# Cross-attention block: scores with keys on partitions, and the maximum subtracted by VectorE and GpSimd in halves

## The chip, the cores and the metric

The kernel runs on one core of a Trainium2 chip. The metric is device time in microseconds (us) from the first to the last instruction of one execution; the median of several runs is compared.

## What is computed

A gated cross-attention block followed by a small mixture of low-rank experts, all in fp32. Eight batches of 56 query tokens attend to 1500 context tokens each; 32 query heads of 128 share 8 key/value heads, four to one.

```python
q = layernorm(x) @ wq                    # (8, 56, 32 x 128), rotary
k = ctx @ wk;  v = ctx @ wv              # (8, 1500, 8 x 128), k rotary; each used by 4 query heads
raw = einsum('bhqd,bhkd->bhqk', q, k) / sqrt(128)
attn = softmax(raw + mask)               # mask (8, 56, 1500)
x = x + tanh(g_xattn) * (attn @ v) @ wo
x = x + tanh(g_ffn) * experts(layernorm(x))
```

## The kernel before

Every fp32 product is made of rounded operands: an operand is split into a high half (ScalarE's copy to fp32r) and a low half (VectorE or GpSimd: the value minus the high half), and three matmul passes, `PASSES`, sum high x high, low x high and high x low. So a matrix that TensorE made and TensorE will read costs one copy on ScalarE and one subtraction on VectorE.

The program has three parts: the queries of all heads (kept in DRAM), the attention, the output and the experts. The attention is 64 steps: batches b of 0 to 7, and in each the key/value heads g of 0 to 7. A step does the softmax and the weighing of its own head, and makes the keys of the next head and values for a pair of heads. The order of the tasks within a step is written out by hand for each engine, in `PE_STEP`, `ACT_STEP` and `DVE_STEP` (lines 66 to 99), for steps of the kinds even, odd, turn (the last head of a batch, which also turns the context of the next batch) and last. The tasks:

- K: keys of the next head, three chunks of 500, on TensorE (L805, 12 matmuls of 500 columns a chunk); ScalarE swaps the halves (swap, L715), VectorE does the rotary cosine, sine and add (cos L938, sin L942, rot L948), ScalarE the high half (L720), GpSimd the low half (`k_low`, L673).
- V: values of two heads, in items of two tiles of 125 keys (L821, 24 matmuls of 256 columns an item), high half on ScalarE (L734), low half on VectorE (L962). An even step does two items, an odd one and the turn four.
- S: scores, the queries as the stationary operand, so that 112 query rows (two heads) lie on partitions and 500 keys on columns: six items of three matmuls (L845). VectorE adds the mask and takes the maximum in one instruction (mask, L1002), reduces the three maxima of a half (max, L1007); ScalarE subtracts the maximum, exponentiates and sums in one instruction over 1500 keys (exp, L760), two a step.
- T: the probabilities have queries on partitions, but weighing needs keys there, so TensorE turns them, six items of four transposes (L857); ScalarE takes the high half (L785) and VectorE the low half (L1027), both from the PSUM bank `t_banks`, a ring of two.
- PV: six items of four matmuls (L874), high values times both halves of the probabilities (448 columns) and low values times the high half (224); ScalarE and VectorE add the two parts (out, L770 and L1033).
- norm: VectorE multiplies by the inverse of the sums (L987), which SyncE has stored to DRAM and loaded back over all partitions; the result goes to `attn`, of two slots, and SyncE stores it.
- C: in the turn, twelve items of four transposes of the next batch's context (L832), high half on ScalarE (L724), low half on VectorE (L953).

Each engine runs its list in order; waits are on semaphores (`t_ready`, `t_free`, `sv_free`, `k_lo` and others). TensorE waits for `k_lo` ahead of scores, `t_free` ahead of turns and of weighing.

## Time and profile before

| | |
|---|---|
| median of 3 runs | 2007.14 us (2006.73 to 2007.7) |
| span of the profiled execution | 2005.4 us |
| TensorE busy | 1976.7 us (99%) |
| VectorE busy | 1235.0 us (62%) |
| ScalarE busy | 1034.3 us (52%) |
| GpSimd busy | 311.6 us (16%) |
| the 64 steps | from 124.0 us to about 1905 us of the span |

In the profile's rows PE is TensorE's matmuls, PEld its weight loads, DVE VectorE, ACT ScalarE, POOL GpSimd and SP SyncE. Matmuls are pipelined, so their busy times overlap, and the distance between two starts is what one costs. The same holds in small for VectorE: the next instruction starts a little before the last one's end. What lies between the span and the profiled execution's full time is not shown; the span is 1.7 us below the median.

### The profile page before, as it was taken

What the parts mean: (1) busy time and instruction counts of PE and PEld (TensorE: products, weight loads), DVE (VectorE), ACT (ScalarE), POOL (GpSimd) and SP (SyncE); (2) the same over time, 40 slices, a digit from 0 to 9 for tenths busy, and PEclk for the clock granted to TensorE, in tenths of its full rate; (3) what the DMA queues carried; (4) which work ended last, traced back from release to release, by engine and by line L of the source; (5) the groups of instructions that cost most, each with busy time, mean ns of one, the idle gap of its engine ahead of it and who ended that gap; (6) DMA issues with size and microseconds to landing.
All of it is one profiled execution on the core that took longest, in us unless ns stands there. A gap on an engine that the chain in (4) does not pass through costs nothing. (4 is left out here: it accounts for less than half of the span.)

```text
span 2005.4 us, 32965 instructions
## 1 busy us (share of the span) xinstructions
PE 1976.7 (99%) x12404; PEld 1775.9 (89%) x12404; DVE 1235.0 (62%) x2639; ACT 1034.3 (52%) x1754; POOL 311.6 (16%) x227
## 2 busy tenths in 40 slices
PE   7999999999999999999999999999999999999998
PEld 7989889988899988998899988998899998999786
DVE  6766556666666666666666666666665666566544
ACT  6655555554545555555644555455554555455532
POOL 5511111111111111111111111111111111111200
PEclk9999999999999999999999999999999999999998
DMA  7611212111211212221111112221111112121270
GB/s 227 248 56 35 35 18 44 35 31 20 43 10 33 36 17 44 35 35 20 39 19 25 35 20 41 36 35 20 39 25 26 28 20 41 36 33 15 48 263 19
DMA packets 74904, 94.41 MB, mean 47 GB/s; under 512 B 22692, under 2 KB 49444, under 8 KB 74760
## 3 DMA queue, kind: packets, MB, share of 16 engines
q1 hardware_dynamic: 73752, 86.01, 20.4%
q10 hardware_dynamic: 1008, 6.42, 0.8%
q8 instruction: 97, 1.59, 0.4%
q14 instruction: 47, 0.39, 0.1%
HBM read 76.64 MB, written 15.77 MB: 46 GB/s over the span
## 5 line engine op out<-in xcount | busy, mean ns | idle before, releaser
L673 POOL TENSOR_TENSOR k_lo<-k_work,k_hi 128x500 fp32r<-128x500 f32 x192 | 244.1, 1285 | 1541.0 <-ACT k_hi L720 1513.3
L821 PE MATMUL low_banks<-wv_hi,cT_hi 128*125 128x256 f32 x1536 | 443.1, 288 | 0.0
L821 PE MATMUL low_banks<-wv_hi,cT_lo 128*125 128x256 f32 x1536 | 431.0, 281 | 0.0
L821 PE MATMUL low_banks<-wv_lo,cT_hi 128*125 128x256 f32 x1536 | 430.9, 281 | 0.0
L1027 DVE TENSOR_TENSOR pT<-t_banks,pT 125x448 fp32r<-125x448 f32 x384 | 236.0, 622 | 242.8 <-ACT pT L785 242.8
L1002 DVE CUSTOM_DVE_ANT_0 prob<-low_banks,mask_t 112x500 f32<-112x500 f32 x384 | 259.1, 678 | 178.2 <-PE low_banks L845 176.9
L785 ACT ACTIVATE pT<-t_banks 125x448 fp32r<-125x448 f32 x384 | 205.1, 543 | 309.2 <-PE t_banks L857 308.2
L760 ACT ACTIVATE prob<-prob,neg_max 112x1500 f32<-112x1500 f32 x128 | 198.6, 1552 | 289.7 <-DVE neg_max L1007 288.9
L805 PE MATMUL low_banks<-cT_hi,wk_hi 128*128 128x500 f32 x768 | 312.0, 406 | 0.0
L805 PE MATMUL low_banks<-cT_hi,wk_lo 128*128 128x500 f32 x768 | 298.6, 389 | 0.0
L805 PE MATMUL low_banks<-cT_lo,wk_hi 128*128 128x500 f32 x768 | 298.3, 388 | 0.0
L821 PEld LDWEIGHTS low_banks<-wv_hi,cT_hi 128*125 128x125 f32 x1536 | 285.1, 186 | 4.3
L821 PEld LDWEIGHTS low_banks<-wv_hi,cT_lo 128*125 128x125 f32 x1536 | 285.8, 186 | 2.7
L821 PEld LDWEIGHTS low_banks<-wv_lo,cT_hi 128*125 128x125 f32 x1536 | 285.2, 186 | 0.0
L874 PE MATMUL o_banks<-pT,v_hi 125*128 125x448 f32 x768 | 272.4, 387 | 1.8 <-DVE pT L1027 0.7
L715 ACT ACTIVATE k_work<-low_banks 64x500 f32<-64x500 f32 x384 | 223.6, 582 | 14.4 <-PE low_banks L805 5.8
L857 PE MATMUL t_banks<-ident,prob 112*125 112x112 f32 x1536 | 220.6, 270 | 0.9 <-DVE pT L1027 0.9
L857 PEld LDWEIGHTS t_banks<-ident,prob 112*125 112x125 f32 x1536 | 207.0, 188 | 14.3 <-DVE pT L1027 1.0
L962 DVE TENSOR_TENSOR v_lo<-low_banks,v_hi 125x512 fp32r<-125x512 f32 x192 | 132.2, 689 | 137.0 <-ACT v_hi L734 137.0
L734 ACT ACTIVATE v_hi<-low_banks 125x512 fp32r<-125x512 f32 x192 | 114.3, 595 | 192.5 <-PE low_banks L821 192.3
L874 PE MATMUL o_banks<-pT,v_lo 125*128 125x224 f32 x768 | 193.5, 265 | 0.0
L805 PEld LDWEIGHTS low_banks<-cT_lo,wk_hi 128*128 128x128 f32 x768 | 144.5, 188 | 29.9
(136 smaller groups left out, 2910.2 us busy)
## 6 DMA issues: line engine op xcount, KB each, us to landing
stage<-in_ctx_dram SPq DMA_DIRECT2D x72, 250.0 KB
attn_by_head<-attn SPq DMA_DIRECT2D x65, 112.0 KB, 1.7
wq_raw<-in_L_xattn_wq_dram SPq DMA_DIRECT2D x7, 1024.0 KB, 7.2
q_raw<-q_by_head SPq DMA_DIRECT2D x64, 112.0 KB, 4.9
inv_b<-inv_by_head SPq DMA_DIRECT2D x64, 112.0 KB, 5.1
head_rows<-in_ctx_dram SPq DMA_DIRECT2D x24, 250.0 KB
mask_t<-in_mask_BxSxS_ff_dram SPq DMA_DIRECT2D x16, 328.1 KB
stage<-in_L_xattn_wo_dram SPq DMA_DIRECT2D x4, 1024.0 KB, 7.3
```

What stands on the lines that cost most here:

```text
L673: nc.gpsimd.tensor_tensor(k[1][:, c * SC:(c + 1) * SC], k_rot[:, s], f32(k[0][:, c * SC:(c + 1) * SC]), ALU.subtract).then_inc(k_lo, 1)
L715: nc.scalar.activation(k_swap[lo * HALF:(lo + 1) * HALF, s], k_banks[(1 - lo) * HALF:(2 - lo) * HALF, s, 0:SC], ACT.Copy).then_inc(k_swapp ...
L734: nc.scalar.activation(v[0][:, 2 * m:2 * m + 2, :], sv_banks[0:ST, m % 2, :].rearrange("p (t n) -> p t n", t=2), ACT.Copy).then_inc(v_hi, 1)
L760: nc.scalar.activation(prob[n][:, :], prob[n][:, :], ACT.Exp, bias=neg_max[:, n:n + 1], accum_out=row_sum[:, n:n + 1]).then_inc(p_ready, 1)
L785: nc.scalar.activation(pT[:, n % PT_SLOTS, :, 0, :], t_banks[0:ST, t_bank, 0:2 * GQ].rearrange("p (t n) -> p t n", t=2), ACT.Copy).then_in ...
L805: mm = nc.tensor.matmul(k_banks[:, s, 0:SC], w[0][a][:, d, g * DH:(g + 1) * DH], cT[m][:, d, c * SC:(c + 1) * SC], start=(d == 0 and n == ...
L821: mm = nc.tensor.matmul(sv_banks[0:ST, m % 2, t * PAIR:(t + 1) * PAIR], cT[a][:, d, tile * ST:(tile + 1) * ST], w[1][mv][:, d, g * DH:g * ...
L857: mm = nc.tensor.transpose(t_banks[0:ST, s, col:col + ROWS], prob[h][:, (2 * j + t) * ST:(2 * j + t + 1) * ST], ident[0:ROWS, 0:ROWS])
L874: mm = nc.tensor.matmul(o_banks[:, g % 2, 0:(2 - a) * GQ], v[a][:, 2 * j + t, (g % 2) * DH:(g % 2 + 1) * DH], probs, start=(first and a == ...
L962: nc.vector.tensor_tensor(v[1][:, 2 * m:2 * m + 2, :], sv_banks[0:ST, m % 2, :].rearrange("p (t n) -> p t n", t=2), f32(v[0][:, 2 * m:2 * ...
L1002: nc.vector.tensor_tensor_reduce(prob[h][:, c * SC:(c + 1) * SC], sv_banks[0:ROWS, n % 2, 0:SC], mask_t[:, c * SC:(c + 1) * SC], 1.0, LOWE ...
L1027: nc.vector.tensor_tensor(pT[:, n % PT_SLOTS, :, 1, :], t_banks[0:ST, t_bank, 0:2 * GQ].rearrange("p (t n) -> p t n", t=2), f32(pT[:, n % ...
```

## The change

Scores are computed with the keys as the stationary operand, so that 125 keys lie on partitions and the 4 x 56 queries on columns. The probabilities come out as weighing needs them, and the turns T are gone. In exchange the maximum and the sum run across partitions.

- Scores: twelve key tiles of three matmuls of 224 columns, two tiles an item, in `t_banks`. VectorE adds the mask out of PSUM into the new SBUF tile `weights`. The mask is turned too (two items B a batch, three transposes each, and a copy by VectorE into `mask_keys`).
- Maximum: VectorE takes it tile by tile (max1 to max5, 448 columns each, both operands in SBUF), then of the two halves (half, 224). TensorE turns the result (MT), VectorE reduces it (rows), TensorE turns it back spread over the partitions (MB), ScalarE copies it to SBUF (maxb).
- Subtraction: six pieces of 448 columns; VectorE does 0 to 2, GpSimd 3 to 5 (`V_SUBS = 3`).
- Exponential on ScalarE, six pieces of 448, without sum. GpSimd adds the pieces up (add1 to add5, total); TensorE turns the sums in the next step (SUM) and VectorE reduces and inverts them (inv).
- High and low halves of the probabilities (T in ScalarE's and VectorE's lists) now read `weights` in SBUF.
- `o_banks` goes from two banks to one, `attn` is gone: `o_sum` is normalised in place and stored, and ScalarE's "out" waits for that store. The values have their own ring (`v_banks`), and weighing counts its pieces in `p_weighed`.
- GpSimd has a list of its own, `POOL_STEP`. The last step's output projection is cut into heads.

The core of the diff:

```diff
 PE_STEP = {
-    "even": ("K00 S0 S1 K01 K02 S2 S3 K03 K10 S4 S5 K11 K12 K13 V40 K20 T0 T1 K21 V41 K22 T2 K23 PV0 V50 T3 PV1 T4 "
-             "V51 PV2 T5 PV3 PV4 PV5"),
+    "even": ("S0 S1 K00 S2 S3 SUM S4 S5 K01 K02 K03 K10 K11 K12 MT K13 MB V40 V41 V50 V51 PV0 K20 K21 K22 PV1 PV2 "
+             "K23 PV3 PV4 PV5"),
...
 ACT_STEP = {
-    "even": "exp0 swap0 exp1 swap1 Q K0 T0 T1 V4 T2 swap2 T3 T4 V5 T5 K1 K2 out",
+    "even": "swap0 Q swap1 maxb exp0 T0 exp1 exp2 T1 V4 T2 V5 exp3 exp4 T3 K0 T4 exp5 T5 swap2 K1 out K2",
...
 DVE_STEP = {
-    "even": ("mask0 mask1 mask2 mask3 max0 mask4 mask5 max1 cos0 sin0 rot0 cos1 T0 T1 sin1 rot1 norm T2 Q V4 inv cos2 T3 "
-             "sin2 T4 rot2 V5 T5 out"),
+    "even": ("mask0 mask1 max1 mask2 mask3 max2 mask4 mask5 max3 max4 max5 half inv rows cos0 Q cos1 sub0 sub1 "
+             "sub2 T0 sin0 sin1 T1 rot0 V4 V5 T2 rot1 T3 T4 T5 norm cos2 sin2 out rot2"),
...
+POOL_STEP = {
+    "odd": "sub3 sub4 sub5 add1 klo0 add2 add3 klo1 add4 add5 total klo2",
+    "even": "sub3 sub4 sub5 add1 add2 add3 add4 klo0 klo1 add5 total klo2",
...
+                if what == "sub":
+                    if j == V_SUBS:
+                        pool.wait_ge(max_copied, n + 1)
+                    nc.gpsimd.tensor_tensor(bank_weights(j), bank_weights(j), max_b[:, None, :].broadcast_to([ST, 2, GQ]),
+                                            ALU.subtract).then_inc(p_shifted, 1)
+                if what == "add":
+                    pool.wait_ge(p_exp, n * PT + (j + 1))
...
+                    nc.gpsimd.tensor_tensor(key_sum[:, :, :], so_far, bank_weights(j), ALU.add).then_inc(p_added, 1)
...
+                if what == "exp":
...
+                    nc.scalar.activation(bank_weights(j), bank_weights(j), ACT.Exp).then_inc(p_exp, 1)
+                if what == "T":
+                    act.wait_ge(p_exp, n * PT + (j + 1))
+                    if n * PT + j >= PT_SLOTS:
+                        act.wait_ge(p_weighed, n * PT + (j + 1 - PT_SLOTS))
+                    nc.scalar.activation(pT[:, j % PT_SLOTS, :, 0, :], bank_weights(j), ACT.Copy).then_inc(p_hi, 1)
...
                 if what == "out":
-                    act.wait_ge(o_ready, b * HKV + (g + 1))
-                    nc.scalar.activation(o_lo[:, :], o_banks[:, g % 2, GQ:2 * GQ], ACT.Copy).then_inc(o_lo_copied, 1)
+                    act.wait_ge(p_weighed, (n + 1) * PT)
+                    act.wait_ge(attn_stored[(n + 1) % 2], 16 * (n // 2 + 2))
+                    nc.scalar.activation(o_sum[:, :], o_bank[:, GQ:2 * GQ], ACT.Copy).then_inc(o_copied, 1)
...
+            for t in range(2):
+                tile = slice((2 * j + t) * ST, (2 * j + t + 1) * ST)
+                for n, (a, m) in enumerate(PASSES):
+                    mm = nc.tensor.matmul(t_banks[0:ST, item % 2, t * GQ:(t + 1) * GQ], k[a][:, tile], q[m][:, :],
+                                          start=(n == 0), stop=(n == len(PASSES) - 1))
...
+            nc.vector.tensor_tensor(bank_weights(j).rearrange(four, h=REP),
+                                    t_banks[0:ST, item % 2, 0:2 * GQ].rearrange("p (t h s) -> p t h s", t=2, h=REP),
+                                    mask_keys[:, j, :, None, :].broadcast_to([ST, 2, REP, SQ]), ALU.add).then_inc(t_free, 1)
...
+            so_far = bank_weights(0) if j == 1 else key_max[:, :, :]
+            nc.vector.tensor_tensor(key_max[:, :, :], so_far, bank_weights(j), ALU.max).then_inc(max_steps, 1)
...
+        def shift(n, j):
+            if j == 0:
+                dve.wait_ge(max_copied, n + 1)
+            nc.vector.tensor_tensor(bank_weights(j), bank_weights(j), max_b[:, None, :].broadcast_to([ST, 2, GQ]),
+                                    ALU.subtract).then_inc(p_shifted_first, 1)
...
                 if what == "T":
-                    dve.wait_ge(t_hi, t_item(b, g, n, last) + 1)
-                    nc.vector.tensor_tensor(pT[:, n % PT_SLOTS, :, 1, :],
-                                            t_banks[0:ST, t_bank, 0:2 * GQ].rearrange("p (t n) -> p t n", t=2),
-                                            f32(pT[:, n % PT_SLOTS, :, 0, :]), ALU.subtract).then_inc(t_free, 1)
+                    dve.wait_ge(p_hi, n * PT + (j + 1))
+                    nc.vector.tensor_tensor(pT[:, j % PT_SLOTS, :, 1, :], bank_weights(j), f32(pT[:, j % PT_SLOTS, :, 0, :]),
+                                            ALU.subtract).then_inc(p_lo, 1)
```

## Rows read from the trace of the kernel before

**Rows 1.** The page, busy time of each engine and its share.
```profile
PE 1976.7 (99%) x12404; PEld 1775.9 (89%) x12404; DVE 1235.0 (62%) x2639; ACT 1034.3 (52%) x1754; POOL 311.6 (16%) x227
```

**Rows 2.** Windows: stretch, us, busy us of PE, PEld, DVE, ACT, POOL, PEclk, DMA share, GB/s.
```profile
682.00:705.90 23.90, 23.86 (x148) 21.23 (x147) 15.85 (x36) 12.94 (x22) 2.80 (x3) 1.00 0.02 6
705.90:736.60 30.70, 30.70 (x202) 28.08 (x202) 17.46 (x39) 14.85 (x26) 4.68 (x5) 1.00 0.22 28
761.30:796.90 35.60, 35.60 (x244) 32.20 (x243) 23.92 (x51) 20.46 (x37) 4.45 (x4) 1.00 0.29 58
572.70:796.90 224.20, 224.06 (x1441) 202.10 (x1440) 139.96 (x309) 117.22 (x204) 30.59 (x25) 1.00 0.17 30
```

**Rows 3.** Timeline of TensorE: start, duration, line, shapes.
```profile
715.02 0.39 PE L805 MATMUL low_banks<-cT_hi,wk_lo 128*128 128x500 f32 x1
715.25 0.39 PE L805 MATMUL low_banks<-cT_lo,wk_hi 128*128 128x500 f32 x1
...
721.53 0.59 PE L857 MATMUL t_banks<-ident,prob 112*125 112x112 f32 x4
721.89 0.36 PE L821 MATMUL low_banks<-wv_hi,cT_hi 128*125 128x256 f32 x1
722.09 0.28 PE L821 MATMUL low_banks<-wv_hi,cT_lo 128*125 128x256 f32 x1
722.21 0.28 PE L821 MATMUL low_banks<-wv_lo,cT_hi 128*125 128x256 f32 x1
...
724.34 0.38 PE L874 MATMUL o_banks<-pT,v_hi 125*128 125x448 f32 x1
724.55 0.27 PE L874 MATMUL o_banks<-pT,v_lo 125*128 125x224 f32 x1
724.65 0.29 PE L821 MATMUL low_banks<-wv_hi,cT_hi 128*125 128x256 f32 x1
```

**Rows 4.** Groups by line and shape: count, busy us, mean ns, idle before; VectorE, ScalarE.
```profile
L1027 DVE TENSOR_TENSOR pT<-t_banks,pT 125x448 fp32r<-125x448 f32 x384 | 236.0, 622 | 242.8 <-ACT pT L785 242.8
L785 ACT ACTIVATE pT<-t_banks 125x448 fp32r<-125x448 f32 x384 | 205.1, 543 | 309.2 <-PE t_banks L857 308.2
L962 DVE TENSOR_TENSOR v_lo<-low_banks,v_hi 125x512 fp32r<-125x512 f32 x192 | 132.2, 689 | 137.0 <-ACT v_hi L734 137.0
L948 DVE TENSOR_TENSOR k_work<-k_work 128x500 f32<-128x500 f32 x192 | 129.6, 675 | 11.6 <-DVE k_work L942 1.9
L1033 DVE TENSOR_TENSOR o_sum<-o_banks,o_lo 128x224 f32<-128x224 f32 x64 | 25.1, 392 | 56.1 <-ACT o_lo L770 56.1
```

**Rows 5.** The same view, GpSimd's instructions of 448 columns.
```profile
L685 POOL TENSOR_TENSOR cT_lo<-head_rows,cT_hi 128x448 fp32r<-128x448 f32 x4 | 4.5, 1151 | 0.0
```

**Rows 6.** Timeline of VectorE and GpSimd around 569 us, and a k_lo that met nothing.
```profile
569.22 0.62 DVE L1027 TENSOR_TENSOR pT<-t_banks,pT 125x448 fp32r<-125x448 f32 x1 [1.85 <-ACT pT L785]
569.76 0.67 DVE L948 TENSOR_TENSOR k_work<-k_work 128x500 f32<-128x500 f32 x1
570.35 0.68 DVE L962 TENSOR_TENSOR v_lo<-low_banks,v_hi 125x512 fp32r<-125x512 f32 x1
...
569.77 1.78 POOL L673 TENSOR_TENSOR k_lo<-k_work,k_hi 128x500 fp32r<-128x500 f32 x1 [10.95 <-ACT k_hi L720]
...
626.81 1.27 POOL L673 TENSOR_TENSOR k_lo<-k_work,k_hi 128x500 fp32r<-128x500 f32 x1 [4.39 <-ACT k_hi L720]
```

**Rows 7.** Timeline of VectorE and GpSimd around 1879 us.
```profile
1879.42 0.90 DVE L948 TENSOR_TENSOR k_work<-k_work 128x500 f32<-128x500 f32 x1
...
1878.49 1.29 POOL L681 TENSOR_TENSOR wk_lo<-stage,wk_hi 128x512 fp32r<-128x512 f32 x1 [7.62 <-ACT wk_hi L1059]
...
1879.73 2.98 POOL L681 TENSOR_TENSOR wk_lo<-stage,wk_hi 128x512 fp32r<-128x512 f32 x2
```

**Rows 8.** DMA issues of the page (KB each, us to landing), and the last step's window.
```profile
attn_by_head<-attn SPq DMA_DIRECT2D x65, 112.0 KB, 1.7
...
1882.20:1905.00 22.80, 18.47 (x84) 14.72 (x84) 10.70 (x22) 8.97 (x11) 8.59 (x8) 0.93 0.44 100
```

More of the change, by code:

```diff
@@ L90 @@
 DVE_STEP = {
[8 rows of a table removed]
[16 rows of a table added]
+}
+POOL_STEP = {
[7 rows of a table added]
 }
 def step_kind(g, last):
-    return ("last" if last else "turn") if g == HKV - 1 else ("odd" if g % 2 else "even")
-def act_kind(g, last):
-    return "pre" if last and g == HKV - 2 else step_kind(g, last)
+    if last and g >= HKV - 2:
+        return "last" if g == HKV - 1 else "pre_last"
+    return ("zero", "odd", "even", "odd", "even", "odd", "pre", "turn")[g]
 def tasks(order):
@@ L706, in _ @@
+        with pool.Fori(0, B - 1) as b:
+            for g in range(HKV):
+                step(b, g, False)
+        for g in range(HKV):
+            step(B - 1, g, True)
     @block.scalar
@@ L869, in weigh @@
+        def weigh(n, j):
+            if j == 0 and n:
+                pe.wait_ge(o_free, n)
+            pe.wait_ge(p_lo, n * PT + (j + 1))
+            if n % 2 == 0:
+                pe.wait_ge(v_free, v_item(n // 2, j) + (RING + 1))
             for t in range(2):
@@ L1178, in _ @@
         with sp.Fori(1, pairs - 1) as i:
-            output_loads(sp, shared, wo, attn_dram, i, sp_passed)
+            for u in range(2):
+                output_load(sp, shared, wo, attn_dram, i, u, sp_passed)
         for t in range(NTT):
```

478 lines of the change are left out of this document (274 added, 204 removed), and 58 rows, old and new, of tables (ACT_STEP, DVE_STEP, PE_STEP, POOL_STEP).

## The prediction

> **What bounds the kernel now.** I read the page's totals first. TensorE is busy 99% of the span, VectorE 62%, ScalarE 52%, GpSimd 16% [rows 1]. Then I cut one batch into its steps [rows 2]: an even step takes 23.9 us, an odd one 30.7 us (it has four projections of V, the even one two), the turn 35.6 us, and a batch 224.2 us, which is 28.0 us a step. In each window TensorE is busy from end to end and VectorE for 16 to 24 us. So TensorE's queue is the bound, and what it saves is worth its full size until another engine takes over. The reader is to ask two things: how much leaves TensorE, and whether VectorE and GpSimd, which receive it, still fit into a step.
>
> **TensorE.** The busy times of the page overlap, so I price matmuls by the distance of their starts [rows 3]. 500 moving columns cost 0.23 us, 448 cost 0.21, 256 cost 0.12 and 224 cost 0.10 to 0.105. Four turns of probabilities take 0.36 us, and the matmul behind them starts 0.08 late (0.20 to the next one instead of 0.12).
> - Removed: six groups of four turns, 6 x 0.44 = 2.64 us a step.
> - Scores: 18 matmuls of 500 columns (4.09 us) become 36 of 224. Two of 224 in a row do not occur before; the bounds are 0.105 (the 224 row) and 0.118 (the 256 row, which loads 125 weight columns too). I take 0.105: 3.78 us, a gain of 0.31; at 0.118 it is a loss of 0.16.
> - Added: three pairs of turns (maximum out, maximum back, sums), each 0.18 + 0.08 = 0.26, together 0.78 us; two pieces of mask a batch, some 0.7 us, 5.6 us in all.
> - Sum: 2.64 + 0.31 - 0.78 = 2.17 us a step. Over 64 steps that is 139 us, less 5.6 = 133. If TensorE stayed the bound, the span of 2005.4 us would become 1872.
>
> TensorE's need is then 21.8 us for an even step, 28.5 for an odd one and 33.5 for the turn.
>
> **ScalarE.** Two exponentials of 1500 columns become six of 448, and six high halves now read SBUF. The row for 448 columns is 543 ns [rows 4]; bounded by that and by VectorE's 622 for the same size, 12 such cost 6.5 to 7.5 us, and with swaps, K, V and the rest ScalarE needs 13 to 15 us. It has room. Its new waits matter more: "out" now waits until the previous attention tile has been stored, because o_sum serves both; K2 is queued behind it, and so is VectorE's "out", with the next step's masks behind that. The store takes 1.7 us from issue to landing [rows 8].
>
> **VectorE, alone.** Its instructions start 0.54 us apart where one lasts 0.62, and 0.59 where one lasts 0.67 [rows 6], so an instruction's price is its mean [rows 4] less 0.08. An even step then has 20 instructions of 448 columns (6 masks, 5 maxima, 3 subtractions, 6 low halves) = 10.8 us; nine of 500 (cosine, sine, add) = 5.3; two of V = 1.2; four of 224 = 1.2; the two reductions of 250 columns lie between the rows for 224 and 448, with the reciprocal 0.8. Together 19.3 us. An odd step has two more of V, 20.5; the turn has twelve context halves (7.1) and two mask copies (0.9) more, 28.5. Taken alone it fits under TensorE.
>
> **GpSimd, alone.** A 448-column instruction takes 1.15 us [rows 5], a k_lo 1.27 [rows 6]. A step now has three subtractions, five adds, one total (half the columns, an estimate of 0.6) and three k_lo: 9.2 + 0.6 + 3.8 = 13.6 us, where before it was 3.8. Alone it fits too.
>
> **VectorE and GpSimd together.** This is the step that decides. In [rows 6] VectorE starts the rotary add (both inputs in SBUF) at 569.76 and GpSimd starts a k_lo at 569.77: that k_lo takes 1.78 us instead of 1.27, so it stood still for 0.51 us, nearly all of VectorE's 0.67. VectorE's next instruction, V's low half with one input in PSUM, runs beside GpSimd at its usual 0.68. In [rows 7] it is the other way round: GpSimd started at 1878.49 and ends at 1879.78, VectorE's add is issued at 1879.42 and takes 0.90 instead of 0.67, then GpSimd's next one, issued at 1879.73, stands until that add is through. So when both read two operands from SBUF one waits for the other, and where both are waiting they alternate. Before, only the rotary sine and add, q_lo and the normalisation could meet a k_lo, and they rarely do: the add's mean is 675 ns, and one pattern a batch shows the 1.78.
>
> The Trainium skill, "SBUF — State Buffer", section "Who interferes with whom", says the same in general: a VectorE instruction with two SBUF inputs contends with a GpSimd instruction that reads SBUF, and whichever starts first keeps the shared port for its whole length. By that rule all the instructions counted next are hit; the two rows of this trace agree.
>
> After the change the instructions of VectorE with two SBUF inputs are 5 maxima, the halving, 3 subtractions, 6 low halves (they read PSUM before), 3 sines, 3 adds, q_lo and the normalisation: 23 a step. By the 0.51 for 500 columns they hold GpSimd off for 14 x 0.46 + 6 x 0.51 + 3 x 0.23 = 10.2 us. GpSimd lets go some 0.14 us ahead of its end (1879.78 less 1879.65, at which the held add must have begun), so its twelve hold VectorE off for 13.6 - 1.7 = 11.9 us. The two sum to 22.1 us, already as long as TensorE's even step, at no idle and no hand-over.
>
> How much falls on VectorE's time depends on what else it does meanwhile. Its work with a PSUM input is 7.3 us, but masks, which are most of it, come before the maximum is known, when GpSimd has nearly nothing ready. From the first subtraction to the end of an even step stand only one cosine, two of V and "out", and with one operation left over into the masks' stretch I let 2.7 us of GpSimd run beside them. The other 9.2 us delay VectorE: 19.3 + 9.2 = 28.5, and 1.0 for waits on ScalarE (out behind the store, the late swap): 29.5 us. Walking the order gives the same: with the maximum spread 10.5 us into the step, eight VectorE instructions alternate with eight of GpSimd at 1.5 us a pair, reach 22.3, and the remaining ten of VectorE with four of GpSimd end near 30. An odd step has 1.2 us more of V as cover, so 20.5 + 8.0 + 1.0 = 29.5, near enough to TensorE's 28.5 that I take 30.3. The turn: 28.5 + 6.0 + 1.5 = 36.0. A batch is 4 x 29.5 + 3 x 30.3 + 36.0 = 245, or 30.6 us a step against 28.0. 64 x 2.6 = 166 us more: 2005.4 + 166 = 2171. The median of the runs shown, 2007.1, lies 1.7 above the span, so 2173.
>
> **DMAs and SyncE.** The order of SyncE's queue changes (the inverse of the sums one step later, the store last, masks in pieces of 500 bytes). VectorE inverts within the first third of a step and normalises in the last, so I cost this at nothing; its cover is that distance. Only the last step normalises ahead of its subtractions; a stall of a few us there, once, lies inside the rounding.
>
> **The rivals.** All are conditions on the same meeting of two engines.
> - Alternating as above, 2173 (2080 to 2290): chance 0.60. For it: both orders of meeting in rows, and 23 + 12 instructions a step that meet.
> - Partly covered: only half of the 9.2 falls on VectorE, since GpSimd idles for exponentials and catches up under V and masks. Even 26, odd 29.2, turn 35: 28.3 a step, 2025. Chance 0.13.
> - Not slower: VectorE's queue is never given up between two of its own, and GpSimd runs only in VectorE's gaps. Then the held time is packed. Place: the stretch behind the spread maximum; price: 22.1 us plus some 2.5 of hand-over and idle, 24.7 for an even step, TensorE's 28.8 and 34 for the others, 27.4 a step, 64 x 0.6 = 40 us less: 1967. It decides from the point where VectorE's delay in an even step falls below 23.9 - 19.3 = 4.6 us, half of what I put. Against it: [rows 7], where GpSimd gets the turn right after VectorE. Chance 0.14.
> - The meeting costs nearly nothing and TensorE stays the bound: 1874. Against it stand the same rows. Chance 0.06.
> - Worse than 2290: waits on the store and on k_lo chain from step to step, and TensorE, waiting a quarter of the time, is granted less clock, as in the stretch that is 81% busy and shows 0.93 [rows 8]. Even 33, odd 33.5, turn 39: 33.9 a step, 2385. Chance 0.07.
> - That the change does not do what it says (no gain on TensorE at all, 0.118 for scores): 0.5 us a step on TensorE, hidden in the forecast since TensorE is not the bound there.
>
> **How the numbers follow.** The likeliest case gives 2173. The range leaves out the 0.06 case, the lower edge of the 1967 case and the case above 2290: 1950 to 2290; the likeliest case's own range is 2080 to 2290. Faster by over 0.2%: 0.14 + 0.06 = 0.20. Within 0.2%, about what measurement can tell from no change: 0.02. Slower: 0.78.
>
> **What would show it.** Right: GpSimd's 448-column instructions with a mean well over 1.15 us, VectorE's maxima, subtractions and low halves well over 0.62 while its masks stay at 0.62; an even step near 29.5 us with VectorE busy nearly throughout; TensorE's busy share near 85 to 90%, its waits ended by VectorE's low halves and masks; four turns gone and score starts 0.105 us apart. Wrong: means at 0.62 and 1.15 and an even step of 22 us (TensorE still bound), or long means only on GpSimd (VectorE keeps the port) and an even step below 25.

## The result and the profile after

| | before | after |
|---|---|---|
| median | 2007.42 us (2006.73 to 2008.94, 4 runs) | 2404.27 us (2403.57 to 2408.71, 4 runs) |
| ratio | | 1.198, 95% interval 1.196 to 1.200 |
| span of the profiled execution | 2005.4 us | 2407.0 us |

Slower by 397 us. The forecast had slower by 166, and 2404 lies above its range (1950 to 2290). The page of the kernel after, busy times and then the granted clock in 40 slices, answers to [rows 1]:

```profile
PE 2044.5 (85%) x12452; PEld 1815.5 (75%) x12452; DVE 2038.5 (85%) x2783; ACT 1059.6 (44%) x1946; POOL 1136.0 (47%) x803
...
PEclk9999999998899999899899999999998999999888
```

TensorE is no longer busy throughout: 85% instead of 99%. But VectorE is at 85% too, so no engine is full over the span, and the waits between them count. The windows of one batch answer to [rows 2] (columns as there: stretch, us, then busy us of PE, PEld, DVE, ACT and POOL, the granted clock, DMA share, GB/s). They are a first step (kind zero), an odd one, an even one, the one before the turn, the turn, and the whole batch:

```profile
674.00:703.30 29.30, 25.58 (x152) 22.89 (x151) 26.70 (x37) 13.79 (x26) 15.11 (x11) 0.88 0.23 41
703.30:738.30 35.00, 30.33 (x200) 27.54 (x199) 30.94 (x43) 15.17 (x29) 19.06 (x14) 0.95 0.15 25
738.30:769.80 31.50, 25.75 (x151) 22.78 (x150) 27.43 (x38) 13.49 (x26) 13.62 (x11) 0.89 0.18 29
868.50:898.80 30.30, 24.62 (x152) 21.31 (x151) 28.72 (x39) 13.47 (x26) 17.13 (x11) 0.95 0.11 12
898.80:947.80 49.00, 39.09 (x253) 34.50 (x251) 35.32 (x53) 21.39 (x41) 16.29 (x13) 0.93 0.07 24
674.00:947.80 273.80, 231.65 (x1448) 206.22 (x1446) 238.82 (x326) 120.74 (x229) 132.80 (x96) 0.93 0.13 23
```

A batch takes 273.8 us, where 245 was forecast and 224.2 was measured before. The 28.8 us too much lie in the turn (49.0 instead of 36.0), in three odd steps (35.0, and near 33.6 for the other two, instead of 30.3) and, least, in the four even ones (30.6 on average instead of 29.5). Not all of the 401.6 us by which the span grew lie in these steps: 383.5 lie between the first step's first score and the last step's. From there to the end the program takes 140.8 us instead of 123.2. The last step has no keys and values to make, and TensorE is busy for 25.6 of its 36.8 us (columns as above):

```profile
2266.20:2303.00 36.80, 25.56 (x115) 22.07 (x113) 24.10 (x27) 12.81 (x18) 26.60 (x20) 0.78 0.37 114
```

Groups by line and shape, from 130 to 1905 us, which is the first 52 steps (count, busy us, mean ns), answer to [rows 4 to 6]:

```profile
L1173 DVE TENSOR_TENSOR pT<-weights,pT 125x448 fp32r<-125x448 f32 x312 | 322.9, 1062 | 11.2 <-ACT pT L818 11.0
...
L722 POOL TENSOR_TENSOR weights<-weights,key_max 125x448 f32<-125x448 f32 x156 | 239.5, 1560 | 581.7 <-ACT key_max L806 581.7
...
L700 POOL TENSOR_TENSOR k_lo<-k_work,k_hi 128x500 fp32r<-128x500 f32 x156 | 226.5, 1453 | 287.9 <-ACT k_hi L767 287.8
...
L1114 DVE TENSOR_TENSOR weights<-weights,key_max 125x448 f32<-125x448 f32 x156 | 200.4, 1331 | 0.0
L1093 DVE TENSOR_TENSOR weights<-t_banks,mask_keys 125x448 f32<-125x448 f32 x314 | 190.1, 618 | 11.7 <-PE t_banks L914 10.6 <-issue 0.3
...
L1041 DVE TENSOR_TENSOR k_work<-k_work 128x500 f32<-128x500 f32 x156 | 165.3, 1060 | 5.0 <-DVE k_work L1035 0.5
...
L1060 DVE TENSOR_TENSOR v_lo<-low_banks,v_hi 125x512 fp32r<-125x512 f32 x156 | 104.4, 679 | 22.2 <-ACT v_hi L784 22.1
```

The low halves of the probabilities have the same 448 columns as before and take 1062 ns instead of 622; the subtraction 1331; the rotary add 1060 instead of 675. All have both inputs in SBUF. The mask (618) and V's low half (679) read one input from PSUM: V's took 689 before, and the mask takes the 0.62 that a low half out of PSUM took. GpSimd's subtraction takes 1560 instead of 1151. That is the forecast's sign of the two engines meeting. In one place the sign is missing: the forecast counted five maxima a step among the instructions that lengthen, and four of them take 627 ns, since GpSimd has little to do while they run; only the first, often beside a late k_lo, takes 984.

The timeline of VectorE and GpSimd in the odd step at 703.3 shows how they share (start, duration; x3 is three instructions in a row):

```profile
717.26 4.56 DVE L1114 TENSOR_TENSOR weights<-weights,key_max 125x448 f32<-125x448 f32 x3
721.74 1.55 DVE L1173 TENSOR_TENSOR pT<-weights,pT 125x448 fp32r<-125x448 f32 x1
723.22 1.73 DVE L1035 TENSOR_TENSOR k_work<-k_work,k_tables 128x500 f32<-128x500 f32 x1
724.87 1.33 DVE L1056 TENSOR_TENSOR q_lo<-q_raw,q_hi 128x224 fp32r<-128x224 f32 x1
726.13 2.08 DVE L1173 TENSOR_TENSOR pT<-weights,pT 125x448 fp32r<-125x448 f32 x2
...
717.10 4.24 POOL L722 TENSOR_TENSOR weights<-weights,key_max 125x448 f32<-125x448 f32 x3 [9.28 <-ACT key_max L806]
721.30 1.51 POOL L730 TENSOR_TENSOR key_sum<-weights 125x448 f32<-125x448 f32 x1
722.77 1.64 POOL L700 TENSOR_TENSOR k_lo<-k_work,k_hi 128x500 fp32r<-128x500 f32 x1
724.37 2.82 POOL L730 TENSOR_TENSOR key_sum<-key_sum,weights 125x448 f32<-125x448 f32 x2
```

From 717.3 to 726 each VectorE instruction starts some 1.5 us after the one before it, and so does each of GpSimd: one of one, one of the other. The small q_lo waits as long as a large one (1.33 us). The Trainium skill, "SBUF — State Buffer", section "Who interferes with whom", says that the pair of ports which the two engines share is an exclusive lock. The trace agrees that the later one stands still until the other lets go, though not quite for the length that the profile gives the other: a pair of 448 columns takes 1.5 us, where 1.15 and 0.62 would be 1.77 (the forecast's terms, 1.15 - 0.14 of GpSimd and 0.46 of VectorE, give 1.47). Who is next when both queue is told by the trace: they alternate.

What TensorE does meanwhile is in its timeline of the same step:

```profile
723.44 0.44 PE L955 MATMUL o_bank<-pT,v_hi 125*128 125x448 f32 x1 [2.53 <-DVE pT L1173]
...
727.73 0.47 PE L955 MATMUL o_bank<-pT,v_hi 125*128 125x448 f32 x1 [2.05 <-DVE pT L1173]
...
729.83 0.41 PE L880 MATMUL low_banks<-wv_hi,cT_lo 128*125 128x256 f32 x1
730.04 0.41 PE L880 MATMUL low_banks<-wv_lo,cT_hi 128*125 128x256 f32 x1
730.26 0.41 PE L880 MATMUL low_banks<-wv_hi,cT_hi 128*125 128x256 f32 x1
...
732.13 0.28 PE L880 MATMUL low_banks<-wv_hi,cT_hi 128*125 128x256 f32 x1
732.25 0.28 PE L880 MATMUL low_banks<-wv_hi,cT_lo 128*125 128x256 f32 x1
```

TensorE waits 2.5 us for the first low half (PV0) and 2.05 for the second (PV1), and only then gets to V2 and V3, 48 matmuls that need nothing of these low halves but stand behind them in its list. Some of them start 0.21 us apart instead of 0.12: after the waits the granted clock is at its lower level, 1.2 GHz. Over the whole trace 380 us of 2407 are at that level, in 69 stretches, about one a step; before it was 18 us.

The turn has a wait of its own. VectorE's timeline, then SyncE's issues:

```profile
910.20 0.17 DVE L1128 RECIPROCAL inv_sum<-row_sum 112x2 f32<-112x2 f32 x1
...
923.65 0.39 DVE L1135 TENSOR_TENSOR o_sum<-o_sum,inv_b 128x224 f32<-128x224 f32 x1 [7.87 <-DMA inv_b<-inv_by_head]
...
910.47 0.33 SPq L636 DMA_DIRECT2D inv_by_head<-inv_sum  x1
919.48 0.35 SPq L638 DMA_DIRECT2D inv_b<-inv_by_head  x1
```

The inverse of the sums is ready at 910.2, its store is issued at 910.5, the load back at 919.5, and the normalisation runs at 923.65: 13.4 us. In the turn the normalisation stands ahead of the maximum's last reduction, so VectorE stands still for 7.9 us, and the maximum, subtraction and exponential of this step with it.

### The profile page after: what moved, and what is told of

Read it like the earlier page. It is cut to its first block and busy times, and to the rows that moved or that the text cites. A ratio compares the mean times of both kernels' runs of the same rounds, so it can differ in the third digit from the quotient of the medians.

```text
span 2407.0 us, 36127 instructions
## 1 busy us (share of the span) xinstructions
PE 2044.5 (85%) x12452; PEld 1815.5 (75%) x12452; DVE 2038.5 (85%) x2783; ACT 1059.6 (44%) x1946; POOL 1136.0 (47%) x803
## 5 line engine op out<-in xcount | busy, mean ns | idle before, releaser
L722 POOL TENSOR_TENSOR weights<-weights,key_max 125x448 f32<-125x448 f32 x192 | 296.1, 1567 | 706.2 <-ACT key_max L806 706.2
L955 PE MATMUL o_bank<-pT,v_hi 125*128 125x448 f32 x768 | 334.1, 463 | 263.6 <-DVE pT L1173 185.1
L1173 DVE TENSOR_TENSOR pT<-weights,pT 125x448 fp32r<-125x448 f32 x384 | 400.9, 1072 | 13.4 <-ACT pT L818 13.1
L730 POOL TENSOR_TENSOR key_sum<-key_sum,weights 125x448 f32<-125x448 f32 x256 | 354.8, 1386 | 34.1 <-ACT weights L812 23.3
L812 ACT ACTIVATE weights<-weights 125x448 f32<-125x448 f32 x384 | 214.7, 572 | 123.3 <-DVE weights L1114 111.3
L818 ACT ACTIVATE pT<-weights 125x448 fp32r<-125x448 f32 x384 | 211.3, 570 | 98.7 <-PE o_bank L955 94.2
L1114 DVE TENSOR_TENSOR weights<-weights,key_max 125x448 f32<-125x448 f32 x192 | 245.4, 1324 | 2.3 <-ACT key_max L806 2.3
L1093 DVE TENSOR_TENSOR weights<-t_banks,mask_keys 125x448 f32<-125x448 f32 x384 | 232.5, 618 | 14.3 <-PE t_banks L914 13.0
L914 PE MATMUL t_banks<-q_hi,k_hi 128*125 128x224 f32 x768 | 222.3, 289 | 4.7 <-DVE q_lo L1056 2.6
L955 PE MATMUL o_bank<-pT,v_lo 125*128 125x224 f32 x768 | 222.6, 304 | 0.0
```

The lines of the kernel that those rows point to most:

```text
L722: nc.gpsimd.tensor_tensor(bank_weights(j), bank_weights(j), max_b[:, None, :].broadcast_to([ST, 2, GQ]), ALU.subtract).then_inc(p_shifted, 1)
L730: nc.gpsimd.tensor_tensor(key_sum[:, :, :], so_far, bank_weights(j), ALU.add).then_inc(p_added, 1)
L812: nc.scalar.activation(bank_weights(j), bank_weights(j), ACT.Exp).then_inc(p_exp, 1)
L914: mm = nc.tensor.matmul(t_banks[0:ST, item % 2, t * GQ:(t + 1) * GQ], k[a][:, tile], q[m][:, :], start=(n == 0), stop=(n == len(PASSES) - 1))
L955: mm = nc.tensor.matmul(o_bank[:, 0:(2 - a) * GQ], v[a][:, 2 * j + t, (n % 2) * DH:(n % 2 + 1) * DH], probs, start=(first and a == 0), sto ...
L1093: nc.vector.tensor_tensor(bank_weights(j).rearrange(four, h=REP), t_banks[0:ST, item % 2, 0:2 * GQ].rearrange("p (t h s) -> p t h s", t=2, ...
```

## Experiments

Each ratio is to the kernel before, run on the same chip (2007.2 to 2008.0 us). All but e9 are edits of the kernel after.

### e1_norm_late: the turn's normalisation behind the second low half

```diff
-             "norm C8 rows cos0 sin0 C9 C10 cos1 sub0 sub1 C11 sub2 sin1 rot0 T0 T1 T2 T3 V0 rot1 V1 T4 T5 cos2 "
+             "C8 rows cos0 sin0 C9 C10 cos1 sub0 sub1 C11 sub2 sin1 rot0 T0 T1 norm T2 T3 V0 rot1 V1 T4 T5 cos2 "
```

> The changed kernel with one task moved: in the turn VectorE normalises behind the second low half instead of ahead of the reduction of the turned maximum. Theory M (the meeting of VectorE and GpSimd, the clock that TensorE loses by waiting, and in the turn the wait for the inverse add up): the turn's wait of 7.9 us for the inverse goes and nothing takes its place, 7 x 8 = 55 us less, about 2349. Rival N (the turn is long for another reason, and its waits move to the next task): under 15 us less, above 2390.

Measured 2357.5 us (1.174, 1.171 to 1.178). The turn takes 43.3 us instead of 49.0, the other steps are as they were, and the normalisation waits for nothing:

```profile
914.04 0.38 DVE L1135 TENSOR_TENSOR o_sum<-o_sum,inv_b 128x224 f32<-128x224 f32 x1
```

So the wait on the inverse cost 47 us in all, 6.7 in each of the seven turns. The next experiments start from this kernel, so that this wait does not hide in them.

### e3_narrow_norm: GpSimd on 8 of 448 columns

It leaves out the subtraction on 440 columns of pieces 3 to 5, and all but 8 columns of the sums. The count of instructions and all waits stay.

```diff
-                    nc.gpsimd.tensor_tensor(bank_weights(j), bank_weights(j), max_b[:, None, :].broadcast_to([ST, 2, GQ]),
+                    nc.gpsimd.tensor_tensor(bank_weights(j)[:, 0, few], bank_weights(j)[:, 0, few], max_b[:, few],
                                             ALU.subtract).then_inc(p_shifted, 1)
```
(The adds and the total in the same way, with `few = slice(0, 8)`; e1's move is in it too.)

> As e1_norm_late, and GpSimd's subtractions, adds and total work on 8 columns instead of 448 (left out: the maximum is not subtracted from three of six pieces and the sums are not formed); order and waits are kept. Theory M: VectorE's two-SBUF instructions return to 0.62, an even step falls to 22 to 24 us, TensorE's clock returns near 1.0, total 1890 to 1960. Rival C (the length comes from the chain of the maximum through the engines, not from the meeting): VectorE's means fall, but steps stay above 28 us, total above 2150.

Measured 1971.7 us (0.982, 0.979 to 0.985). Its page and, of its groups, low half, rotary add and subtraction:

```profile
PE 1884.9 (96%) x12452; PEld 1702.0 (86%) x12452; DVE 1648.3 (84%) x2785; ACT 1044.4 (53%) x1946; POOL 591.7 (30%) x803
```
```profile
L1176 DVE TENSOR_TENSOR pT<-weights,pT 125x448 fp32r<-125x448 f32 x384 | 248.8, 674 | 27.0 <-ACT pT L819 25.7
...
L1044 DVE TENSOR_TENSOR k_work<-k_work 128x500 f32<-128x500 f32 x192 | 167.6, 873 | 5.8
...
L1117 DVE TENSOR_TENSOR weights<-weights,key_max 125x448 f32<-125x448 f32 x192 | 110.1, 620 | 2.6 <-ACT key_max L807 2.6
```

With little meeting left (k_lo's, which the rotary add's 873 ns still shows) even steps are bound by TensorE again, at a granted clock of 0.992 over the span: even step 22.8 us, odd 28.8 to 31.1, turn 39.0. GpSimd's 440 columns are worth 2357.5 - 1971.7 = 386 us. That holds the meeting, the waits and the clock that it brings, and one thing more which e3 can't tell from them: GpSimd's own subtraction is short too (598 ns instead of 1151 undisturbed), so the exponentials behind it can start earlier. e5 and e8 below move the work instead of leaving it out. e3 is 36 us faster than the kernel before, where TensorE's saving was forecast at 133: of the 35 us between the two profiled spans, 53 are gained between the first and the last step's first score, 16.5 are lost behind it and 1.8 ahead. The even step is 1.0 longer than the forecast's TensorE sum of 21.8, and the turn 5.5 longer than its 33.5.

### e5_subs6 and e6_subs0: the six subtractions on one engine

```diff
-V_SUBS = 3
+V_SUBS = 6
```
(e5; the three names sub3 to sub5 move from GpSimd's lists to VectorE's. e6 has `V_SUBS = 0` and the reverse. Both with e1's move.)

> As e1_norm_late, with all six subtractions on VectorE (V_SUBS = 6): 1.6 us more on VectorE, 3.45 us less on GpSimd a step. Theory M: three GpSimd instructions fewer to meet, 3 x 1.0 less against 1.6 more, so 0 to 2 us a step less, 2230 to 2349. Rival C (the chain behind the maximum sets the step, and halves on two engines shorten it): 2380 or more.

> As e1_norm_late, with all six subtractions on GpSimd (V_SUBS = 0). Theory M: three GpSimd instructions more to meet against 1.6 us less on VectorE, and the first exponential waits 1.15 us instead of 0.6: the mirror of e5_subs6, which was 83 us faster than e1_norm_late, so 2400 to 2460. Rival (it is the overlap of the two engines in the subtractions alone that costs; with all on GpSimd VectorE does other work meanwhile): 2357 or less.

Measured 2274.3 us for e5 (1.133, 1.125 to 1.141) and 2394.8 for e6 (1.193, 1.189 to 1.196). Giving VectorE three more instructions takes 83 us off; taking its three away adds 37. VectorE's low half takes 897 ns in e5 and 1371 in e6, so its means follow GpSimd's work in these runs. The split in halves is no balance: for the time of both, a piece is dearer on GpSimd. e6 came out a little below what was expected of it.

### e8_all_vector: subtractions, adds and total on VectorE

GpSimd keeps only k_lo.

```diff
+                if what == "add":
+                    dve.wait_ge(p_exp, n * PT + (j + 1))
...
+                    nc.vector.tensor_tensor(key_sum[:, :, :], so_far, bank_weights(j), ALU.add).then_inc(p_added, 1)
```

> As e1_norm_late, with all subtractions, adds and the total on VectorE; GpSimd keeps k_lo alone. 11 x 0.54 minus three already there = 4.6 us more on VectorE a step than in e1_norm_late, and nothing but three k_lo to meet. Theory M: an even step is VectorE's 19.3 + 4.6 + 1 to 2 for k_lo = 25 to 26.5, odd 29.5 to 31, turn 41 to 43: 2020 to 2120, the fastest of the versions that compute everything, and still not faster than before. Rival (two engines are needed, since VectorE alone is too long): above 2274, where e5_subs6 stood.

Measured 2177.9 us (1.085, 1.082 to 1.088). It is the fastest version that computes everything, and 58 us above what was expected. The even steps (25.7 to 26.3 us) and the turns (near 41) came as expected; the odd ones take 31.1 to 34.2 where 29.5 to 31 were expected. Its page:

```profile
PE 1948.2 (89%) x12452; PEld 1731.4 (80%) x12452; DVE 1937.9 (89%) x3359; ACT 1052.2 (48%) x1946; POOL 373.7 (17%) x227
```

The means are back (low half 648 ns, subtraction 685), but VectorE now has 3359 instructions and is 89% busy, and an even step takes more than before's 23.9. So without a meeting the work is too much for VectorE, and with one it is too much for the pair.

### e9_before_gpsimd: the kernel before, with sixteen unread additions on GpSimd a step

224 columns each, both inputs in SBUF, none of them read.

```diff
+                    for k in range(6 if c < 2 else 4):
...
+                        nc.gpsimd.tensor_tensor(spare[:, :], f32(w[1][0][0:ST, 0, 0:GQ]), f32(w[1][1][0:ST, 0, 0:GQ]),
+                                                ALU.add).then_inc(spare_done, 1)
```

> The kernel before, with 16 additions of 224 columns a step on GpSimd, both inputs in SBUF, that nobody reads (10 us a step, as in the changed kernel). Theory M: VectorE's instructions with one input in PSUM (mask L1002, low half L1027, cosine L938, V L962) keep their 0.62 to 0.69; its sine, add, q_lo and normalisation rise by 0.2 to 0.6; k_lo comes later; since TensorE has 8 to 13 us a step of VectorE's slack, total at most 2 to 4% up, 2010 to 2090. Rival (any load on GpSimd slows all of VectorE): L1027 and L1002 above 0.75, total above 2150.

Measured 2231.8 us (1.112, 1.108 to 1.115). Its groups:

```profile
L701 POOL TENSOR_TENSOR spare<-wv_hi,wv_lo 125x224 f32<-125x224 f32 x1008 | 713.6, 708 | 64.2
...
L1034 DVE TENSOR_TENSOR pT<-t_banks,pT 125x448 fp32r<-125x448 f32 x384 | 235.8, 621 | 213.8 <-ACT pT L792 213.8
...
L852 PE MATMUL low_banks<-k_hi,q_hi 128*112 128x500 f32 x384 | 163.3, 425 | 185.6 <-POOL k_lo L675 185.6
...
L955 DVE TENSOR_TENSOR k_work<-k_work 128x500 f32<-128x500 f32 x192 | 137.4, 715 | 11.6 <-DVE k_work L949 1.9
L969 DVE TENSOR_TENSOR v_lo<-low_banks,v_hi 125x512 fp32r<-125x512 f32 x192 | 131.9, 687 | 133.4 <-ACT v_hi L741 133.4
```

With GpSimd busy for 714 us more, the instructions with an operand in PSUM keep their 621 and 687 ns, and only those with two in SBUF lengthen (rotary add 715 from 675, normalisation 630 from the 389 ns of the kernel before). So it depends on the operands, and not on GpSimd being busy. The total lies where the rival had it (above 2150), but the rival's sign, low half and mask above 0.75, is absent. It rose otherwise than through VectorE: k_lo queues behind the unread additions, and TensorE's scores wait 185.6 us for it, once a step.

### e4_filler and e7_fit_filler: unread matmuls in TensorE's waits

What does the lower clock cost? TensorE gets matmuls that nobody reads, so that it does not idle. e4 has 42 of 256 columns in every step (12 ahead of PV0, 10 ahead of PV1, PV2 and PV3); e7 has them only where e1's trace shows a wait.

```diff
+FILL = {'zero': {0: 26}, 'odd': {0: 16}, 'even': {0: 12, 2: 20}, 'pre': {3: 10, 4: 18}, 'pre_last': {3: 10, 4: 18}, 'turn': {0: 18}}
...
+            for _ in range(FILL.get(kind, {}).get(j, 0)):
+                nc.tensor.matmul(m_bank[:, 256:512], w[1][0][:, 0, 0:DH], w[1][0][:, 0, 0:PAIR], start=True, stop=True,
+                                 skip_group_check=True)
```

> As e1_norm_late, with matmuls of 256 columns that nobody reads ahead of PV0 (12) and PV1, PV2, PV3 (10 each), 42 of 0.12 us, so that TensorE works while it waits for low halves. Theory M with a large share of the clock: granted clock above 0.98, and total 40 to 100 us below e1_norm_late in spite of 5 us more of matmuls a step. Rival D (the clock costs little, VectorE alone sets the step): clock up, total equal to e1_norm_late or up to 100 us more.

> As e1_norm_late, with matmuls of 256 columns that nobody reads, only where and as long as its TensorE waits: 26 ahead of PV0 in step zero, 16 in odd, 12 and 20 (PV2) in even, 10 and 18 (PV3, PV4) in pre, 18 in the turn. Theory M: granted clock from 0.93 to above 0.98; in e4_filler the same even step took 30.2 us without and 31.7 with a stretch of 3.4 us at the lower clock, so 0.7 to 1.5 us a stretch, one to two stretches a step, 45 to 120 us less: 2240 to 2310. Rival D (VectorE alone sets the step): 2340 to 2370.

e4 took 2409.3 us (1.200, 1.197 to 1.203; mean granted clock 0.981), 52 more than e1. That is what rival D had: the clock up, and the total equal or up to 100 us more. The extra matmuls were themselves in the way in the odd steps (35.5 us), though a pre step fell from 30.3 to 28.1. e7 took 2342.3 (1.167, 1.163 to 1.170), also at 0.981: only 15 us less than e1. This too lies in rival D's range (2340 to 2370), where 45 to 120 less had been expected if the clock were large. But D's reason, that VectorE alone sets the step, does not hold for every kind. The same even step of e1 and of e7:

```profile
720.20:751.60 31.40, 25.66 (x151) 22.67 (x151) 27.50 (x38) 13.47 (x26) 14.59 (x12) 0.89 0.18 28
738.90:768.00 29.10, 26.34 (x180) 23.70 (x180) 27.18 (x38) 11.87 (x22) 14.05 (x11) 1.00 0.10 20
```

An even step has no low stretch left and takes 29.0 us instead of 31.3; a pre step takes 29.2 instead of 30.3 and a turn 42.2 instead of 43.1. Zero steps gain nothing, and two of three odd steps take 35 to 36 us, two more than in e1. In one of these GpSimd's work of the step before reaches further in, and VectorE's first low half starts 19.6 us into the step instead of 18.4; whether the unread matmuls bring that about was not tried.

### e10 to e13: what sets an odd step

The forecast had VectorE's 29.5 and TensorE's 28.5 and took 30.3; measured were 33.5 to 35. Four orders of the same work, none of which leaves anything out. First TensorE's list (K22 and K23 ahead of PV0; e11 also V20 and V21 ahead of PV2, with V0's copies earlier):

```diff
-"odd": ("... MB V01 V10 V11 PV0 K22 K23 PV1 PV2 V20 V21 V30 V31 PV3 PV4 PV5"),
+"odd": ("... MB V01 V10 V11 K22 K23 PV0 PV1 PV2 V20 V21 V30 V31 PV3 PV4 PV5"),   # e10
+"odd": ("... MB V01 V10 V11 K22 K23 PV0 PV1 V20 V21 PV2 V30 V31 PV3 PV4 PV5"),   # e11
```

> The kernel after with the late normalisation (e1_norm_late, 2357.5 us, odd steps 33.5 to 34.7) and one change: in the odd steps K22 and K23, six matmuls of 500 columns that stood between PV0 and PV1, stand ahead of PV0. That is 6 x 0.23 = 1.4 us of TensorE's work put into its 2.8 us wait for the first low half. Theory A (TensorE's list is run in order and work that stands behind a wait is added to it, so a wait in mid-list lengthens the odd step although no engine is busy throughout): PV0's wait shrinks by 1.4; PV1's grows by what the low half of T1 is still missing (T1 comes 1.1 to 2.1 us behind T0), so 0.3 to 1.0 us a step are gained, odd steps 32.9 to 33.6, total 2335 to 2350. Rival B (the chain over VectorE, busy 31 of 33.8 us, sets the odd step): odd steps unchanged, 2354 to 2361.

> As e10_keys_first, and V20 and V21 (24 matmuls of 256 columns, 2.9 us) ahead of PV2 too; for that the copies of V0 go ahead of the high and low half of T2 on ScalarE and VectorE. Theory A: the waits at PV1 and PV2 (0.8 to 1.9 us in e1_norm_late) are filled as well, odd steps 31.5 to 32.8, total 2305 to 2335. Rival B: VectorE's list, longer ahead of T2 by one instruction of V, sets the step: odd steps 33.5 to 34.5, total 2350 to 2375.

Measured 2391.9 us (1.192, 1.190 to 1.194) and 2411.6 (1.201, 1.199 to 1.203): 34 and 54 slower than e1. No range had that: one theory had a gain, the other nothing in e10 and at most 18 us in e11. The step at 686.8 of e1 and the one at 697.0 of e10, TensorE's weighing:

```profile
706.57 0.44 PE L955 MATMUL o_bank<-pT,v_hi 125*128 125x448 f32 x1 [2.57 <-DVE pT L1173]
...
707.57 0.65 PE L863 MATMUL low_banks<-cT_hi,wk_hi 128*128 128x500 f32 x1
...
710.86 0.47 PE L955 MATMUL o_bank<-pT,v_hi 125*128 125x448 f32 x1 [0.56 <-DVE pT L1173]
```
```profile
721.12 0.74 PE L955 MATMUL o_bank<-pT,v_hi 125*128 125x448 f32 x1 [3.41 <-DVE pT L1173]
721.65 0.39 PE L955 MATMUL o_bank<-pT,v_lo 125*128 125x224 f32 x1
721.84 0.61 PE L955 MATMUL o_bank<-pT,v_hi 125*128 125x448 f32 x1
```

PV1 starts 24.1 us into the step in both (710.86 - 686.8, 721.12 - 697.0). In e1 K22 and K23 had filled most of the time to it; part of them ran at the lower clock (0.65 us), which cost nothing, since PV1 was not ready. (In 17 of e1's 24 odd steps these slow matmuls just fill the time: PV1 follows them at 23.7 to 24.5 without a wait, and PV2 waits some 0.5 us for its own low half.) In e10 TensorE idles 3.4 us instead, and the lower clock now falls on PV1 and PV2 (0.61 us where it is 0.37 at full clock), behind which the rest of the list waits. In 17 of e10's 24 odd steps TensorE is at the lower clock for twice as long as in the rest, in e1 in 3 of 24, and e10's odd steps take 34.4 to 36.6 us. Over the whole run e10 has 392 us at the lower clock and e1 has 313.5; half of the 78.5 more, 39 us, is what they can cost (an estimate), and e10 is 34 us slower. e11 is not explained so: it has 352 us at the lower clock, and its even and pre steps became 0.8 and 0.9 us longer too, for which no run gives the cause. I had taken T1's low half to come 1.1 to 2.1 us behind T0's; it comes 4.4 behind, since between them stand a rotary sine and q_lo, both in the alternation (the same pair as 723.22 and 724.87 of the timeline above).

So that moment was moved, in VectorE's list:

```diff
-"odd": ("... sub1 sub2 T0 sin1 Q T1 T2 rot1 V0 T3 V1 norm T4 T5 ..."),
+"odd": ("... sub1 sub2 T0 T1 T2 V0 sin1 Q T3 V1 rot1 norm T4 T5 ..."),     # e12 and e13
-"even": ("... sub2 T0 sin0 sin1 T1 rot0 V4 V5 T2 rot1 T3 T4 T5 norm ..."),
+"even": ("... sub2 T0 T1 T2 sin0 sin1 V4 V5 rot0 T3 rot1 T4 T5 norm ..."),  # e13
```

> The kernel after with the late normalisation (e1_norm_late, 2357.5 us) and one change, in VectorE's list of the odd steps: the low halves of T1 and T2 and V0's go ahead of the rotary sine and q_lo. In e1_norm_late and e10_keys_first alike T1's low half ends 24.0 us into the odd step, and TensorE's PV1 starts at 24.1 whatever TensorE has done before; what is left of its list then takes 9.4 us (33.5). Theory A (an odd step is that moment plus the rest of TensorE's list): T1's low half ends 2.9 us earlier, at 21.1; the work between PV0 and PV1 then fills until 22.2, and the odd step ends at 31.0 to 32.0. 24 steps x 2.2 = 53 us: 2290 to 2320. Rival B (the sum of VectorE's list, 31 us busy, sets the step, and its order is of no account): 2350 to 2362.

> As e12_odd_turns, and the same in the even steps: the low halves of T1 and T2 ahead of the two sines, the values and the rotary add. In e1_norm_late TensorE waits there for T1's low half until 21.5 and for T2's until 25.6 us. Theory A: T2's ends near 20.9 to 22.3, PV2 starts 3 us earlier, even steps 28.5 to 29.8 instead of 31.3; 24 steps in both kinds together: 2235 to 2285. Rival B: VectorE's 27.4 us busy and its waits on ScalarE keep the even step at 30.5 to 31.5, total as e12_odd_turns within 10 us.

Measured 2319.1 us for e12 (1.155, 1.153 to 1.157) and 2304.9 for e13 (1.148, 1.146 to 1.150). The odd step at 679.3 of e12, its window, VectorE's low halves and TensorE's PV2:

```profile
679.30:710.70 31.40, 28.66 (x200) 26.16 (x199) 30.51 (x42) 15.00 (x29) 18.14 (x13) 1.00 0.16 28
```
```profile
697.70 4.65 DVE L1173 TENSOR_TENSOR pT<-weights,pT 125x448 fp32r<-125x448 f32 x3
...
702.40 0.47 PE L955 MATMUL o_bank<-pT,v_hi 125*128 125x448 f32 x1 [0.15 <-DVE pT L1173]
```

VectorE is busy for 30.5 us (31.0 before the move), but the three low halves are done 23.1 us into the step, TensorE waits once for long (2.5 us, ahead of PV0), PV1 starts at 22.2 as theory A had it, the clock stays at 1.00, and the step takes 31.4 us instead of 33.5. The other two odd steps of a batch take 32.0 to 34.4, above the 31.0 to 32.0 that were expected: there K22 and K23 fall on the lower clock, and PV1 comes mostly at 23.1 to 23.7. e12 is 38 us faster than e1, at the low end of what theory A gave (37 to 67), and rival B is out. Less time at the lower clock is not the cause of that gain: e1 and e12 have 313.5 and 313.6 us of it, and the two kinds of odd step that mostly keep their time at it still gain 1.6 and 1.2 us on average (the first kind, which mostly loses its low stretch, 2.4). What the stretches fall on differs between the two, so a part of the gain may still come that way. But where the low halves stand in VectorE's list counts, at nearly equal busy time. The step shown leaves little more to gain by order, since VectorE is busy for 30.5 of its 31.4 us.

In the even steps the same move brought 1.2 us (31.3 to 30.1), and e13 lies between its two ranges, 14 us below e12: the wait went from PV2 to PV3, which waits 1.0 to 2.6 us now, and PV4 0.7 to 1.3 more.

## Why the prediction was wrong in size

The direction and the mechanism of the meeting were right. What failed is the way from the engines' busy sums to the length of a step: waits were priced at 1.0 us in an even step, 1.8 in an odd one and 1.5 in the turn, and the wait for the inverse at nothing. In the batch shown VectorE is busy for 238.8 us, near the forecast's 234.0 (four even and three odd steps at 28.5, the turn at 34.5). But it is idle for 35.0 us where the forecast had 10.9, and 24 of the 28.8 us too much are that: 13.7 idle in the turn, 4.1 in an even and in an odd step.

**TensorE's saving** (2.17 us a step, 133 in all). Partly right: four turns gone, and scores start 0.108 us apart where 0.105 was taken. But e3 shows 36 us of it. The needs by kind of step were also cut in the wrong place. The windows of the kernel before go from first score to first score, and there K00 of an even step stands ahead of its first score, as do C0 and C1 of the turn. So the 23.9 us of an even step lack three matmuls of its own (0.7 us), which the 30.7 and the 35.6 hold. By its own tasks an even step needed 24.6 and needs 22.8 in e3: a saving of 1.8. The turn's 33.5 holds that 0.7 too much, and lacks C0 and C1 (0.8) and the two pieces of the mask (0.7, counted in the 133); put right it is 34.3, and in e3 TensorE is busy for 35.6 of 39.0 us. The error mattered little for the forecast, since TensorE was not to be the bound, but the rival at 1874 took the whole 133.

**The meeting** (which instructions, in what manner, how much falls on VectorE). Right in kind. Only instructions with two SBUF inputs lengthen; e9 shows it in the kernel before. They alternate at 1.5 us a pair, as forecast. Means of after less those of before put 7.4 us on VectorE in an even step (9.2 forecast) and 8.7 to 9.6 in an odd one (8.0 forecast). That one came out too high and the other too low, so that their sum fits, is luck in part; so is that the maxima, counted but hardly hit, did no harm. e3, e5 and e6 show the direction and bound the size: 386 us at most for GpSimd's share of columns, 83 less and 37 more for three pieces moved either way. The rival "GpSimd runs only in VectorE's gaps" is excluded by the timeline.

**From engine sums to a step.** This is the step that failed. "20.5 + 8.0 + 1.0 = 29.5, near enough to TensorE's 28.5 that I take 30.3" takes the larger of two sums and adds 0.8. TensorE's list is in order, and in an odd step 20 weighing matmuls and the 48 of V stand behind a wait for T1's low half (in most odd steps of e1, T2's). In the step of e1 that was shown, its length is the moment of that low half (24.1 us) plus what is left in TensorE's list (9.4 us): 33.5. e12 shows it: with that moment earlier and VectorE's work the same, the step is shorter. e10 shows the other half: with the moment unmoved nothing is gained, and what is left in the list becomes longer by the clock. With three odd steps a batch at 3.3 to 4.7 us too much that is 11 of the 28.8 us. Walking VectorE's order would have given that moment: the forecast walked it for an even step, but only to its end, and not to the low halves.

**The inverse** ("costed at nothing; its cover is that distance"). Wrong for the turn. The distance from inverting to normalising was taken as two thirds of a step; in the turn's list VectorE normalises before the maximum's last reduction, and the inverse is back from its store and load only 13.4 us behind the reciprocal. The forecast had named only the last step for this. e1: 47 us in seven turns, 5.7 of the 13.0 in the turn shown (49.0 less 43.3). Of the rest, 4.3 us are what e3 takes away (43.3 less 39.0), which the forecast had inside its 36.0, and the size of e3's turn itself was not foreseen: 39.0 is above VectorE's 28.5 and TensorE's 33.5 (34.3). There TensorE waits 3.3 us for VectorE's masks and context halves, which share a ring of two banks with the scores; the other 1.3 us, TensorE's 35.6 less 34.3, were not taken apart.

**Waits** (1.0 us an even step). Too small. VectorE is busy for 27.4 of 31.5 us; the sum before the waits (28.5) was near, but 4.1 us of idle stand behind it. In e7, at full clock, VectorE is busy for 27.2 of 29.1. So some 2 us of an even step come back to TensorE's clock; that slow matmuls make the next masks late is the likely way, and was not tried by itself. A wait that the forecast did not price stands beside it: ScalarE's high half of V waits for the weighing that frees its slot, 153.8 us in all, with exponentials queued behind it. What that wait costs no run shows. What the clock costs in all is not settled either. e7 gave 15 us net: by kind of step, even, pre and turn gain some 50 us and the odd ones lose some 34, so 15 is a lower end. An upper end, an estimate from e1's 313.5 us at half the clock, is 157 us; where TensorE waits afterwards anyway (e1's K22 and K23) a low stretch costs nothing.

**The rival nearest the time** was "Worse than 2290" (2385, chance 0.07). Half of its mechanism is there: TensorE waits and is granted less clock, 0.92 over the span. That belonged in the sum, since the forecast itself had TensorE waiting part of the time. The other half, waits on the store and on k_lo that chain from step to step, is not: it had 39 us for the turn, which takes 49, and 33 for the even step, which takes 31.5. That it is only 19 us off is luck in part.

**The last step** was forecast as one like the others, 2.6 us longer. From its first score to the end the program is 17.6 us longer, and 16.5 in e3, so GpSimd's columns are not the reason. Which of its waits is, no run shows.

**The store of the attention tile** behind "out", which the forecast priced among the waits: VectorE's "out" waits 34 us in all for ScalarE, half a microsecond a step. It stayed inside the forecast's 1.0.

No order tried here comes near the kernel before. The best that computes everything is e8, at 1.085. e12's order was not tried together with e8's.

## To carry to other kernels

Before work goes from the busiest engine to two idle-looking ones, count on both the instructions that take two operands from SBUF: here VectorE's and GpSimd's ran like one queue, at 1.5 us a pair of 448 columns, and half shares on the two were no balance. Then don't compare sums of engines: walk each list to the moment at which the in-order engine needs a result, and add what stands behind it in that list. A round trip through DRAM has a length (13.4 us from reciprocal to use here); look in each kind of step at whether the distance is there, the odd one out above all.
